# Attention scores on two halves of the array's rows, the mask inside the exponents' product, and products that stream 99 columns

## The reference, cut to what matters

```python
log_fg = jax.nn.log_sigmoid(fgate_preact[..., 0])
cs = jnp.cumsum(log_fg, axis=-1)
fg_mat = cs[..., :, None] - cs[..., None, :]
mask = jnp.tril(jnp.ones((S, S), dtype=bool))
log_D = jnp.where(mask, fg_mat + igate_preact[..., 0][..., None, :], -jnp.inf)
max_log_D = jnp.max(log_D, axis=-1, keepdims=True)
D = jnp.exp(log_D - max_log_D)
k_scaled = k / jnp.sqrt(jnp.float32(DH)).astype(k.dtype)
qk = jnp.einsum('bhsd,bhtd->bhst', q, k_scaled)
C = qk * D
normalizer = jnp.maximum(jnp.abs(jnp.sum(C, axis=-1, keepdims=True)), jnp.exp(-max_log_D))
C_norm = C / (normalizer + EPS)
return jnp.einsum('bhst,bhtd->bhsd', C_norm, v)
...
scores = jnp.einsum('btd,ed->bte', x, gate_w)
topk_scores, topk_idx = jax.lax.top_k(scores, TOP_K)
```

## Time and profile before

| what | value |
|---|---|
| runs (us) | 723.02, 711.88, 732.9; median 723.02 |
| profiled execution | 712.25 us, its span 710.2 us, mean granted clock 0.908 |
| PE busy | 611.6 us (86%) |
| DVE busy | 472.2 us (66%) |
| ACT, POOL busy | 315.4 us (44%), 306.1 us (43%) |

### The profile page before, as it was taken

One profiled execution on the slowest core, in us unless ns is written; L12 is line 12 of the kernel. 1 busy time (PEld: TensorE's weight loads), 2 busy tenths in 40 slices (PEclk: granted clock), 3 DMA queues, 4 the chain that ended last, 5 costly groups with the idle time before them and its releaser, 6 DMA issues.

```text
span 710.2 us, 14836 instructions
## 1 busy us (share of the span) xinstructions
PE 611.6 (86%) x3464; PEld 477.1 (67%) x3481; DVE 472.2 (66%) x1039; ACT 315.4 (44%) x704; POOL 306.1 (43%) x312
## 2 busy tenths in 40 slices
PE   3873699999999999512499999999999999999993
PEld 1331366677667677401388888888888888888883
DVE  3664358567558658899366776676767777667673
ACT  3454445345345335200255555555555455555551
POOL 2323443634533633200245455554554545545442
PEclk9998699889779889555699999999999999999998
DMA  8995555555635543360123333323333333233331
GB/s 274 293 298 174 169 142 161 176 151 160 187 116 173 168 135 117 104 243 7 40 38 56 59 53 53 60 46 59 52 53 60 48 57 55 50 60 50 55 45 23
DMA packets 71674, 76.67 MB, mean 108 GB/s; under 512 B 12959, under 2 KB 63781, under 8 KB 71653
## 3 DMA queue, kind: packets, MB, share of 16 engines
q1 hardware_dynamic: 55652, 50.18, 22.7%
q0 software_dynamic: 15712, 25.73, 19.6%
q10 hardware_dynamic: 288, 0.52, 0.2%
HBM read 53.20 MB, written 23.21 MB: 108 GB/s over the span
## 4 chain that ended last, share of the span: by engine, by line
issue 36%; PE 26%; POOL 13%; DVE 11%; DMA 9%; ACT 2%; SPq 1%; POOLq 0%; DVEq 0%; ACTq 0%
POOL xg L1080 9%; PE bank L1167 8%; PE bank L1181 7%; DMA out_rows<-ys,index 5%; POOL out_rows L1089 4%; DMA qT_scratch<-qt 3%; PE bank L1162 3%; PE bank L1164 2%; DVE ohn L933 2%; PE bank L1230 2%; DVE ohp L932 1%; PE bank L1198 1%; DVE wabs L813 1%; PE bank L1207 1%; PE bank L1132 1%
## 5 line engine op out<-in xcount | busy, mean ns | idle before, releaser
L1089 POOL DMA_INDIRECT out_rows<-ys,index x71 | 113.8, 1602 | 155.0 <-DVE ys L985 152.9
L1267 PE MATMUL bank<-w12l,xh 128*128 x284 | 120.8, 425 | 2.2 <-DVE xl L957 2.2
L1268 PE MATMUL bank<-w12h,xl 128*128 x284 | 112.7, 397 | 0.0
L1269 PE MATMUL bank<-w12h,xh 128*128 x284 | 112.6, 396 | 0.0
L991 DVE TENSOR_TENSOR w3l<-w,w3h 128x1024 fp32r<-128x1024 f32 x71 | 87.2, 1228 | 31.0 <-issue 30.0
L1080 POOL DMA_INDIRECT xg<-token_table,index x71 | 70.4, 991 | 74.6 <-DVE index L950 52.9
L1181 PEld LDWEIGHTS bank<-aug,c 128*128 128x128 f32 x512 | 73.8, 208 | 34.6 <-issue 29.8
L781 DVE SCALAR_TENSOR_TENSOR c<-bank,d 128x512 f32<-128x512 f32 x64 | 44.2, 690 | 65.5 <-PE bank L1181 57.1
L655 ACT CAST w3h<-w 128x1024 fp32r x71 | 74.4, 1048 | 20.1 <-issue 20.1
L1295 PE MATMUL bank<-w3l,hth 128*128 128x256 f32 x284 | 76.4, 301 | 1.8 <-DVE w3l L991 1.8
L1167 PE MATMUL bank<-qbd,kt 128*128 128x512 f32 x128 | 74.8, 669 | 3.2 <-issue 3.2
(11 more groups left out here) (164 smaller groups left out, 1083.0 us busy)
## 6 DMA issues: line engine op xcount, KB each, us to landing
x<-in_x SPq DMA_DIRECT2D x32, 256.0 KB, 3.2
wst<-in_w12T POOLq DMA_DIRECT2D x26, 256.0 KB, 3.6
aug<-in_ctxv SPq DMA_DIRECT2D x16, 264.0 KB, 2.9
ct<-in_ctxT SPq DMA_DIRECT2D x16, 256.0 KB, 4.4
qT_scratch<-qt SPq DMA_DIRECT2D x16, 256.0 KB, 3.8
kt<-in_ctxT SPq DMA_DIRECT2D x16, 256.0 KB
qbd<-qT_scratch SPq DMA_DIRECT2D x64, 64.0 KB
out_rows<-x SPq DMA_DIRECT2D x16, 256.0 KB, 2.2
```

Source lines behind the costliest of these rows:

```text
L1089: q.indirect_dma_start(out=out, out_offset=bass.IndirectOffsetOnAxis(ap=index[:, j:j + 1], axis=0), in_=YS[o][:], in_offset=None, compute_ ...
L1267: mm(acc, XH[i][:, k, :], wl, start=(k == 0), stop=False)
L1268: mm(acc, XL[i][:, k, :], wh, start=False, stop=False)
L1269: ins = mm(acc, XH[i][:, k, :], wh, start=False, stop=(k == NK - 1))
```

## The change

- S(n) is cut in two: rows 0 to 63 of `KT` and `QBD` (two heads) give 256 columns into bank 2, rows 64 to 127 (the other two heads) give 256 columns into bank 3. Both banks now belong to one group, so S(n) waits for C(n-1) instead of C(n-2). C(n) reads both banks in one operation of the same size.
- E(n) loses the mask product. `LG` and `RM` get 65 more rows (92 in all) with the mask in them: 64 rows that hold an indicator of the key against a masked triangle, and one row for keys that lie in the other half of the chunk. Since the 64 rows cover 64 query positions, E(n) is two products of 256 columns, one for each half of the queries.
- V(n) streams 99 columns for each head instead of 33: its own and those of the two heads after it, which the next products overwrite (at the end of a sequence there are fewer columns left: 66 and 33).
- The router's products stream 99 columns instead of 8, of which 91 are zeros.
- `LG` is loaded twice for each sequence (two copies side by side), and the constants of `LG`, `RM` and `gate_w` are larger; `id_b` and `mask4` are gone.

```diff
+HALF = P // 2
+GROWS = PARTS * (NH + 1)
+MROWS = GROWS + HALF + 1
...
-        bank = [stack.enter_context(nc.psum_tensor(f"bank{i}", [P, 512], F32)) for i in range(8)]
+        bank = [stack.enter_context(nc.psum_tensor(f"bank{i}", [P, 512], F32)) for i in range(2)]
+        bank23 = stack.enter_context(nc.psum_tensor("bank23", [P, 2, 512], F32))
+        bank += [bank23[:, 0, :], bank23[:, 1, :]]
+        bank += [stack.enter_context(nc.psum_tensor(f"bank{i}", [P, 512], F32)) for i in range(4, 8)]
...
-        RM = [sb(f"rm{i}", [PARTS * (NH + 1), NH, S], BF16, on=early) for i in range(2)]
-        LG = [sb(f"lg{i}", [PARTS * (NH + 1), S], BF16, on=early) for i in range(2)]
+        RM = [sb(f"rm{i}", [MROWS, NH, S], BF16, on=early) for i in range(2)]
+        LG = [sb(f"lg{i}", [MROWS, 2, S], BF16, on=early) for i in range(2)]
...
-                for dst, src in ((ib, ibias), (fb, fbias), (id_b, identb), (mask4, maskT), (io, iota)):
+                for dst, src in ((ib, ibias), (fb, fbias), (io, iota)):
...
                 for i in range(2):
-                    sp.dma_start(LG[i][0:PARTS, :], marks[0:PARTS, 0:S]).then_inc(late_consts, 16)
-                    sp.dma_start(RM[i][PARTS:PARTS * (NH + 1), :, :],
-                                 marks[PARTS:PARTS * (NH + 1), :].rearrange("q (h s) -> q h s", h=NH)
+                    for lo, hi in ((0, PARTS), (GROWS, MROWS)):
+                        sp.dma_start(LG[i][lo:hi, :, :], lgc[lo:hi, :].rearrange("q (a s) -> q a s", a=2)
+                                     ).then_inc(late_consts, 16)
+                    sp.dma_start(RM[i][PARTS:, :, :], rmc[PARTS:, :].rearrange("q (h s) -> q h s", h=NH)
                                  ).then_inc(late_consts, 16)
...
-                    sp.dma_start(LG[i][PARTS:, :], g_dram[b].rearrange("q h s -> (q h) s")).then_inc(in3[i], 16)
+                    for a_ in range(2):
+                        sp.dma_start(LG[i][PARTS:GROWS, a_, :], g_dram[b].rearrange("q h s -> (q h) s")
+                                     ).then_inc(in3[i], 16)
...
-                        v.scalar_tensor_tensor(C[n % 2][:], bank[2 + n % 2][:], KS, D[n % 2][:],
+                        v.scalar_tensor_tensor(C[n % 2][:].rearrange("p (r q) -> p r q", r=2), bank23[:, :, 0:2 * P],
+                                               KS, D[n % 2][:].rearrange("p (r q) -> p r q", r=2),
                                                ALU.mult, ALU.mult).then_inc(c_ready, 1)
...
-                    mm(bank[n % 2][:], LG[i][:, c * P:(c + 1) * P],
-                       RM[i][:, hg * HG:(hg + 1) * HG, c * P:(c + 1) * P], start=True, stop=False)
-                    mm(bank[n % 2][:], id_b[:], mask4[:], start=False, stop=True).then_inc(e_ready, 1)
-
-                    wait(pe, c_ready, k - 1)
-                    mm(bank[2 + n % 2][:], KT[i][:, hg, c * P:(c + 1) * P],
-                       QBD[i][:, hg, :, c * P:(c + 1) * P], start=True, stop=True).then_inc(s_ready, 1)
+                    for a_ in range(2):
+                        at = c * P + a_ * HALF
+                        ins = mm(bank[n % 2][:].rearrange("p (h q) -> p h q", h=HG)[:, :, a_ * HALF:(a_ + 1) * HALF],
+                                 LG[i][:, a_, c * P:(c + 1) * P],
+                                 RM[i][:, hg * HG:(hg + 1) * HG, at:at + HALF], start=True, stop=True)
+                    ins.then_inc(e_ready, 1)
+
+                    wait(pe, c_ready, k)
+                    for r_ in range(2):
+                        rows_ = slice(r_ * 2 * DH, (r_ + 1) * 2 * DH)
+                        ins = mm(bank23[:, r_, 0:2 * P], KT[i][rows_, hg, c * P:(c + 1) * P],
+                                 QBD[i][rows_, hg, r_ * 2:(r_ + 1) * 2, c * P:(c + 1) * P], start=True, stop=True)
+                    ins.then_inc(s_ready, 1)
...
-                        ins = mm(bank[4 + c][:, h * DV:(h + 1) * DV], C[n % 2][:, j * P:(j + 1) * P],
-                                 AUG[vi][:, c, h, :], start=True, stop=True)
+                        wide = min(WIDE, (NC - c) * NH - h) * DV
+                        at = (c * NH + h) * DV
+                        ins = mm(bank[4 + c][:, h * DV:h * DV + wide], C[n % 2][:, j * P:(j + 1) * P],
+                                 AUG[vi][:].rearrange("p c h d -> p (c h d)")[:, at:at + wide], start=True, stop=True)
...
-                            ins = mm(bank[6][:, at:at + NE], X2T[:, c * NK + k, :], gate_w[:, k, :],
+                            ins = mm(bank[6][:, at:at + WIDE * DV], X2T[:, c * NK + k, :], gate_w[:, k, :],
                                      start=(k == 0), stop=(k == NK - 1))
```

More of the change, by code:

```diff
@@ L44 @@
 DV = DH + 1
+WIDE = 3
 N = B * S
@@ L76, in then, with build @@
         self.eng.wait_ge(self.sem, self.base + self.n)
-def build(nc, x, ctx, ctxv, ctxT, gkq, gkk, gkv, ibias, fbias, onw, w12T, w3T, gateT, ident, identb,
-          maskT, trib, marks, iota, iota16, codes, floors, spares, out):
+def build(nc, x, ctx, ctxv, ctxT, gkq, gkk, gkv, ibias, fbias, onw, w12T, w3T, gateT, ident, lgc, rmc, trib, iota, iota16, codes, floors, spares, out):
     qT_dram = nc.dram_tensor("qT_scratch", (B, P, NG, S), F32).ap()
@@ L107, in build @@
         id_f = sb("id_f", [P, P])
-        id_b = sb("id_b", [P, P], BF16)
         tri = sb("tri", [P, 2, P], BF16)
         io = sb("io", [P, P])
-        gate_w = sb("gate_w", [P, NK, NE])
+        gate_w = sb("gate_w", [P, NK, WIDE * DV])
         scores = sb("scores", [P, NT, NE])
@@ L122, in build @@
         onwb = sb("onwb", [P, NH, DH], on=early)
-        mask4 = sb("mask4", [P, HG * P], BF16, on=early)
         wst = [sb(f"wst{i}", [P, HID], on=early) for i in range(2)]
@@ L324, in build @@
         K1 = 2 * NC
-        LOADS3 = 1 + HG + 2
+        LOADS3 = 1 + HG + 3
         LOADSV = 3
@@ L1325 @@
     token = p + P * np.arange(NT)[None, :]
-    marks = np.ones((PARTS * (NH + 1), NH * S), np.float32)
-    marks[PARTS:] = np.tile(np.repeat(np.eye(NH), S, axis=1), (PARTS, 1))
+    key, row = np.arange(S) % P, np.arange(HALF)[:, None]
+    lgc = np.ones((MROWS, 2, S), np.float32)
+    lgc[GROWS:MROWS - 1] = np.stack([key[None] == row, key[None] == row + HALF], axis=1)
+    lgc[MROWS - 1] = np.stack([key >= HALF, np.zeros(S)])
+    rmc = np.full((MROWS, NH, S), MASKED, np.float32)
+    rmc[PARTS:GROWS] = np.tile(np.eye(NH)[:, :, None], (PARTS, 1, S))
+    rmc[GROWS:MROWS - 1] = np.where(row > np.arange(S) % HALF, MASKED, 0.0)[:, None]
     ins = {
@@ L1339 @@
         "w3T": a["w3"].transpose(2, 0, 1).reshape(KH, P, NE, E).transpose(1, 2, 0, 3).reshape(P, -1),
-        "gateT": a["gate"].T.reshape(NK, P, NE).transpose(1, 0, 2).reshape(P, -1),
+        "gateT": np.concatenate([a["gate"].T.reshape(NK, P, NE).transpose(1, 0, 2),
+                                 np.zeros((P, NK, WIDE * DV - NE), np.float32)], axis=2).reshape(P, -1),
         "ident": np.eye(P, dtype=np.float32),
-        "identb": np.eye(P).astype(bf),
-        "maskT": np.tile(np.where(p > q, MASKED, 0.0), (1, HG)).astype(bf),
+        "lgc": lgc.reshape(MROWS, -1).astype(bf),
+        "rmc": rmc.reshape(MROWS, -1).astype(bf),
         "trib": np.concatenate([p < q, np.ones((P, P))], axis=1).astype(bf),
-        "marks": marks.astype(bf),
         "iota": np.broadcast_to(q, (P, P)).astype(np.float32),
```

## The result

The changed kernel is slower: its runs took 743.77, 748.16, 747.24 and 757.02 us, median 747.7, against 722.65 for the kernel before (four runs, 711.88 to 732.9). Ratios, here and in the table further down, leave out the runs that are over 1.5% above the fastest of their kernel; this one is 1.041, with a 95% interval of 1.021 to 1.060 (the two medians alone give 1.035). I had forecast 704 and gave "slower" 0.08. The prediction was wrong.

The account below looks back on a forecast made before the run. PE was taken as the bound (11.40 of 11.56 us a step). Profiled 712.25 - 19.3 (clock falls gone) + 13 x 0.15 + 2.8 + 2.0 + 2.0 + 0.4 = 702.1, plus 1.9 for the median's gap: 704 us, range 691 to 723.

Parts of the forecast that it names:

- "slower": Rival: waits ahead of S(3) and S(1) leave the clock low in many steps, 742 us and above; chance 0.08.
- waits of 0.69 and 1.03 us walked: In each attention step PE waits for C, 0.69 us ahead of S(1) and 1.03 ahead of S(3).

Follow-up runs that it names:

- e11: Changed kernel with `RM` constants loaded in three transfers and S as one 128-row product, still waiting for C(n-1): median 708.7 us, 0.988 of before.
- e6: Changed kernel with `RM` constants in three transfers, S whole with the old wait, V and router at 33 and 8 columns: median 714.9 us, 0.989 of before.
- e1: Changed kernel with the 89 constant rows of `RM` loaded as three transfers of 24, 64 and 1 rows: median 730.3 us, 1.027 of before.
- e10: Kernel before with V and router streaming 99 columns, nothing else changed: median 698.5 us, 0.973 of before.

## What to carry to other kernels

Before a transfer gets a new number of rows, factor the number: 89 rows cost 26 us, 96 rows and more bytes next to nothing. A change that makes PE's products shorter has to be weighed with the clock: list what each product streams before and after, not only how long it occupies PE, and test the padding (V and router wide) apart from the restructuring, since here the first alone gave 23 us and the second gave them away. A single-buffered bank pair turns every hidden latency of the consumer into a wait of the producer, and here that could be walked from the trace of before to about a tenth of a microsecond (waits of 0.69 and 1.03 us walked, 0.57 and 1.12 measured).

## What the runs showed of the hardware

- A load of 89 rows of 4 KB runs on one DMA engine of 16 at 26 to 27 GB/s, and what is queued behind it waits: one later transfer's issue took SP 12.5 us, and a load of x kept DVE waiting for 31.2.
- Idle time alone doesn't tell whether TensorE's clock falls here. e11 had PE waiting up to 1.5 us at a time, 1.6 to 2.7 in each step, and stood at 2.4 GHz from 92 to 265 us; e6, with narrow V and router, fell behind every wait of 0.68 us and then ran at a granted 0.59 for a step of 16.55 us in which PE was never idle. e11 and e1 are busy for the same share of a full-clock step (10.61 of 12.31, 10.06 of 11.85) and only one keeps its clock. What separates them in PE's work is S: 0.86 us on all rows against 0.63 in halves.
- The Trainium skill (TensorE: Matmul & The Clock Gate, HAM oscillation — how this bites in real kernels) puts falls down to gaps in which PE waits for a DMA. In this kernel that isn't the whole cause: e6 falls behind waits of 0.68 us for ACT, and e11 doesn't fall behind waits of 1.5 us for DVE.
- Columns that nobody reads can pay: e10 gives PE 0.38 us more work in a step and saves 23 us.
- Two products of 64 rows run side by side all the way, f32 passes too (0.63 us for the group at 256 columns, 1.06 at 512), with 0.20 us fixed for the group and 0.09 to 0.10 us for each change between half and full rows.
